# A decoder layer's feed-forward: the last batch in two halves of its tokens, and the previous norm's variance between two units of the projection up

## What is computed

```python
def _layernorm(x, axis=-1, eps=1e-05):
    m = jnp.mean(x, axis=axis, keepdims=True)
    v = jnp.var(x, axis=axis, keepdims=True)
    return (x - m) / jnp.sqrt(v + eps)
...
h = _bitlinear(x, w_fc) + gate * (x @ v.T @ fast_b.T @ u.T)
r = jnp.maximum(h, 0.0)
return _bitlinear(r * r, w_proj)      # w_proj rounded to -1, 0, 1, with one scale for each output row
...
x = _layernorm(x + _L0_ffn_ref(x, ...), axis=-1)
```

## Time and profile before

| | |
|---|---|
| device time, median of 3 runs (lowest, highest) | 1326.9 us (1326.89, 1328.72) |
| time of the profiled execution | 1323.5 us |
| span of its trace | 1321.6 us |
| busy in the span: PE, DVE, ACT, POOL | 1270.6, 923.3, 792.9, 776.1 us |
| granted TensorE clock, mean | 0.988 of full speed |

### The profile page before, as it was taken

One profiled execution on the slowest core, in us unless ns is written; L12 is line 12 of the kernel. 1 busy time (PEld: TensorE's weight loads), 2 busy tenths in 40 slices (PEclk: granted clock), 3 DMA queues, 4 the chain that ended last, 5 costly groups with the idle time before them and its releaser, 6 DMA issues.

```text
span 1321.6 us, 21020 instructions
## 1 busy us (share of the span) xinstructions
PE 1270.6 (96%) x6800; PEld 846.9 (64%) x6800; DVE 923.3 (70%) x1802; ACT 792.9 (60%) x1058; POOL 776.1 (59%) x449
## 2 busy tenths in 40 slices
PE   6999999999999999999999999999999998899995
PEld 4767765657566666756665666666666664677773
DVE  6578876684775777476667757675765678678885
ACT  2353445575666566565656655565666556688983
POOL 3504218994877787677868767794876779200000
PEclk9999999999999999999999999999999999999997
DMA  6301211100200110010011001100100100101100
GB/s 213 112 32 64 82 47 19 19 2 17 50 4 1 32 34 0 16 32 18 0 32 34 0 16 32 18 0 21 44 2 1 48 17 1 48 32 48 48 32 32
DMA packets 99118, 43.07 MB, mean 33 GB/s; under 512 B 77152, under 2 KB 81520, under 8 KB 99072
## 3 DMA queue, kind: packets, MB, share of 16 engines
q1 hardware_dynamic: 98256, 39.33, 11.9%
q0 software_dynamic: 816, 3.15, 0.7%
HBM read 29.59 MB, written 12.58 MB: 32 GB/s over the span
## 4 chain that ended last, share of the span: by engine, by line
PE 89%; POOL 3%; DVE 3%; ACT 2%; issue 1%; SPq 1%; DMA 1%; POOLq 0%; ACTq 0%; DVEq 0%
PE ps L1310 16%; PE ps L1285 14%; PE ps L48 11%; PE ps L50 10%; PE ps L49 10%; PE ps L1301 4%; PE ps L1289 4%; PE ps L1342 2%; PE ps L1344 2%; PE ps L1343 2%; PE ps L1660 2%; PE ps L1661 2%; PE ps L1319 2%; POOL acc L931 2%; PE ps L716 1%
## 5 line engine op out<-in xcount | busy, mean ns | idle before, releaser
L1139 DVE CUSTOM_DVE_ANT_0 junk<-ps,mask 128x512 bf16<-128x512 f32 x504 | 314.9, 686 | 89.1 <-PE ps L1301 87.8
L1005 ACT ACTIVATE prob<-ps,mcol 128x1024 f32<-128x1024 f32 x256 | 281.9, 1116 | 139.5 <-PE ps L1289 134.5
L931 POOL TENSOR_TENSOR acc<-acc,prob 128x1024 f32<-128x1024 f32 x128 | 306.9, 2398 | 11.5
L928 POOL TENSOR_TENSOR acc<-prob 128x1024 f32<-128x1024 f32 x64 | 155.3, 2426 | 219.7 <-ACT prob L1005 218.4
L1310 PE MATMUL ps<-prob,v_b 128*64 128x512 f32 x1024 | 245.0, 599 | 0.2 <-ACT prob L1005 0.2
L945 POOL TENSOR_TENSOR acc_lo<-acc,acc_hi 128x1024 f16<-128x1024 f32 x64 | 138.7, 2167 | 5.1
L1310 PEld LDWEIGHTS ps<-prob,v_b 128*64 128x64 f32 x1024 | 67.9, 137 | 108.1 <-issue 74.9
L1285 PE MATMUL ps<-q_hi,k_hi 64*128 64x512 f32 x512 | 114.8, 444 | 4.2 <-DVE rs L225 4.0
L1301 PE MATMUL ps<-k_hi,q_hi 64*128 64x512 f32 x504 | 100.9, 395 | 3.8 <-DVE nmx L1139 3.8
L1289 PE MATMUL ps<-shift,ones_r 64*128 64x512 f32 x512 | 102.1, 394 | 0.1
L1285 PE MATMUL ps<-q_lo,k_hi 64*128 64x512 f32 x512 | 102.1, 394 | 0.0
(11 more groups left out here) (213 smaller groups left out, 2869.2 us busy)
## 6 DMA issues: line engine op xcount, KB each, us to landing
shift<-nmx SPq DMA_DIRECT2D x512, 0.5 KB, 2.0
x_in<-in_xT SPq DMA_DIRECT2D x8, 512.0 KB, 3.6
x_scratch<-x_a SPq DMA_DIRECT2D x8, 512.0 KB, 2.8
raw<-in_cT SPq DMA_DIRECT2D x8, 512.0 KB, 3.6
raw<-x_scratch SPq DMA_DIRECT2D x8, 512.0 KB, 3.8
y<-x_scratch SPq DMA_DIRECT2D x8, 512.0 KB, 3.7
y_scratch<-y SPq DMA_DIRECT2D x8, 512.0 KB, 2.8
y_c<-y_scratch SPq DMA_DIRECT2D x8, 512.0 KB, 3.8
```

What stands on the lines that cost most here:

```text
L928: pool.tensor_tensor(total, prob[:, 0], prob[:, 1], ALU.add).then_inc(acc_out, 1)
L931: pool.tensor_tensor(total, total, prob[:, kt], ALU.add).then_inc(acc_out, 1)
L1005: act.activation(prob[:, i].rearrange("p h t -> p (h t)"), SCORE[i % 2].rearrange("p h t -> p (h t)"), ACT.Exp, scale=SCALE, bias=mcol[:, ...
L1139: dve.tensor_tensor_reduce(junk[:, t % 2, h], SMAX[t % 2][:, h], mask[:], -1.0, -LOWEST, ALU.add, ALU.min, nmx[:, p % 2, t, h:h + 1]).then ...
```

## The change

In the last batch alone:

- `var3(b - 1)` moves on PE from between the tiles of `project` to between `hidden` 6 and 7, `norm3_root(b - 1)` on ACT to between the units 6 and 7, and the root's part on DVE (`root3`, split off from `normalise3`) to before the last h_lo. The output x3 of batch 6 (`scale3`) stays behind it.
- `project` works on two halves of 256 tokens: twice as many matmuls (64), each of 256 columns and with its own weight load. The early half writes the first 256 columns of the banks in OUT, the late half the last 256 columns of the banks HIDDEN[0] and HIDDEN[1]. The order is: early, both groups, tiles 0 to 5; late, group 0, tiles 0 to 5; early, tiles 6 and 7; late, group 1, tiles 0 to 5; late, tiles 6 and 7.
- The norm of the last batch is made for each half: residual, sum, mean, deviation, squares (now on ACT, not DVE), their sum, variance, root, output, and a store of 256 KB for each half. The statistics of the early half go to bank 0, those of the late half to bank 5.

For all other batches the order of every engine stays what it was.

```diff
@@ sync
-        for b in range(B - 4, B):
+        for b in range(B - 4, B - 1):
             store(b)
-        sp.wait_ge(f.stored, 16 * B)
+        for j, cols in enumerate(HALVES):
+            sp.wait_ge(x3_out, B + j)
+            sp.dma_start(batch_cols(out, B - 1)[:, :, cols], x3[:, :, cols]).then_inc(f.stored, 16)
+        sp.wait_ge(f.stored, 16 * (B + 1))
@@ scalar, batch
-            for i in (6, 7):
-                hidden(b, i, first)
-            if not first:
+            hidden(b, 6, first)
+            if last:
+                norm3_root(b - 1, second)
+            hidden(b, 7, first)
+            if not (first or last):
                 norm3_root(b - 1, second)
@@ scalar, end
-        norm3_root(B - 1, False)
+        def last_squares(j, cols):
+            act.wait_ge(dev3_out, B + j)
+            act.activation(sq3[:, :, cols], dev3[:, :, cols], ACT.Square).then_inc(sq3_out, 1)
...
+        for j, cols in enumerate(HALVES):
+            last_squares(j, cols)
+        for j, cols in enumerate(HALVES):
+            last_root(j, cols)
@@ vector, batch
             hidden_lo(b, 6)
...
+            if last:
+                root3(b - 1)
             hidden_lo(b, 7)
...
+            if not (first or last):
+                root3(b - 1)
             if not first:
-                normalise3(b - 1, second)
+                scale3(b - 1, second)
@@ vector, end
+        early, late = HALVES
+        last_residual(0, early)
+        last_deviation(0, early)
+        last_residual(1, late)
+        last_sum_squares(0, early)
+        last_deviation(1, late)
+        last_sum_squares(1, late)
+        last_normalise(0, early)
+        last_normalise(1, late)
@@ tensor
+        def project_half(j, m, tiles):
+            for k in tiles:
+                pe.wait_ge(f.lo_out, HK * (B - 1) + k + 1)
+                w = f.tern[:, k, m * P:(m + 1) * P]
+                pe.matmul(LAST_OUT[j][m], w, h_hi[:, k, HALVES[j]], start=(k == 0), stop=False)
+                mm = pe.matmul(LAST_OUT[j][m], w, h_lo[:, k, HALVES[j]], start=False, stop=(k == HK - 1))
+            if tiles[-1] == HK - 1:
+                mm.then_inc(f.p_ps, 1)
@@ tensor, batch
+            hidden(b, par, 6, first)
+            if last:
+                var3(b - 1)
+            hidden(b, par, 7, first)
...
+            if last:
+                pe.wait_ge(f.relu_out, HK * b + 6)
+                for m in range(DK):
+                    project_half(0, m, range(0, 6))
+                project_half(1, 0, range(0, 6))
+                for m in range(DK):
+                    project_half(0, m, (6, 7))
+                project_half(1, 1, range(0, 6))
+                for m in range(DK):
+                    project_half(1, m, (6, 7))
@@ tensor, end
-        mean3(B - 1, False)
-        var3(B - 1)
+        for j, cols in enumerate(HALVES):
+            pe.wait_ge(y3_sum_out, B + j)
+            if j == 1:
+                pe.wait_ge(rs3_out, 2 * (B - 1))
+            pe.matmul(LAST_STAT[j], c["mean_w"][:], y3_sum[:, cols], start=True, stop=True).then_inc(mean3_ps, 1)
+        for j, cols in enumerate(HALVES):
+            pe.wait_ge(sq3_sum_out, B + j)
+            pe.matmul(LAST_STAT[j], c["mean_w"][:], sq3_sum[:, cols], start=True, stop=True).then_inc(var3_ps, 1)
```

More of the change, by code:

```diff
@@ L1470, in ffn_phase @@
     y3, dev3, sq3, x3, y3_sum, sq3_sum = f.y3, f.dev3, f.sq3, f.x3, f.y3_sum, f.sq3_sum
+    HALVES = (slice(0, T // 2), slice(T // 2, T))
+    LAST_STAT = tuple(bank[:, cols] for bank, cols in zip((STAT2, STAT3), HALVES))
+    LAST_OUT = tuple([bank[:, cols] for bank in banks] for banks, cols in zip((OUT, HIDDEN[:2]), HALVES))
     @block.sync
@@ L1536, in _, with last_root @@
         batch(B - 1, 1, False, False, True)
-        norm3_root(B - 1, False)
+        def last_squares(j, cols):
+            act.wait_ge(dev3_out, B + j)
+            act.activation(sq3[:, :, cols], dev3[:, :, cols], ACT.Square).then_inc(sq3_out, 1)
+        def last_root(j, cols):
+            est, inv, done = f.est3[:, cols], f.inv3[:, cols], 3 * (B - 1 + j)
+            act.wait_ge(var3_ps, B + j)
+            if j == 0:
+                act.wait_ge(rs3_out, 2 * (B - 1))
+            act.activation(inv, LAST_STAT[j], ACT.Ln, bias=c["eps"][:, 0:1]).then_inc(est3_out, 1)
+            act.wait_ge(est3_out, done + 1)
+            act.activation(est, inv, ACT.Exp, scale=-0.5).then_inc(est3_out, 1)
+            act.wait_ge(est3_out, done + 2)
+            act.activation(inv, est, ACT.Square).then_inc(est3_out, 1)
+        for j, cols in enumerate(HALVES):
+            last_squares(j, cols)
+        for j, cols in enumerate(HALVES):
+            last_root(j, cols)
     @block.vector
@@ L1574, in deviate3, with root3, scale3 @@
                               ALU.subtract).then_inc(dev3_out, 1)
-        def normalise3(b, first):
+        def root3(b):
             f.inverse_root(dve, STAT3, (f.est3, f.inv3, f.rs3), est3_out, rs3_out, b)
+        def scale3(b, first):
             if not first:
@@ L1623, in _, with last_residual, last_deviation, last_sum_squares @@
         batch(B - 1, 1, False, False, True)
[L1624 to L1628, removed]
+        def last_residual(j, cols):
+            for m in range(DK):
+                dve.wait_ge(f.p_ps, 2 * (B - 1 + j) + m + 1)
+                if j == 0 and m == 0:
+                    dve.wait_ge(dev3_out, B - 1)
+                dve.scalar_tensor_tensor(out=y3[:, m, cols], in0=LAST_OUT[j][m], scalar=pscale[:, m:m + 1],
+                                         in1=f.x2[:, 1, m, cols], op0=ALU.mult, op1=ALU.add).then_inc(f.y3_out, 1)
+            dve.wait_ge(f.y3_out, 2 * (B + j))
+            if j == 0:
+                dve.wait_ge(mean3_ps, B - 1)
+            dve.tensor_tensor(y3_sum[:, cols], y3[:, 0, cols], y3[:, 1, cols], ALU.add).then_inc(y3_sum_out, 1)
+        def last_deviation(j, cols):
+            dve.wait_ge(mean3_ps, B + j)
+            if j == 0:
+                dve.wait_ge(x3_out, B - 1)
+            mean = LAST_STAT[j].rearrange("p (o t) -> p o t", o=1).to_broadcast([P, DK, T // 2])
+            dve.tensor_tensor(dev3[:, :, cols], y3[:, :, cols], mean, ALU.subtract).then_inc(dev3_out, 1)
+        def last_sum_squares(j, cols):
+            dve.wait_ge(sq3_out, B + j)
+            if j == 0:
+                dve.wait_ge(var3_ps, B - 1)
+            dve.tensor_tensor(sq3_sum[:, cols], sq3[:, 0, cols], sq3[:, 1, cols], ALU.add).then_inc(sq3_sum_out, 1)
+        def last_normalise(j, cols):
+            f.inverse_root(dve, LAST_STAT[j], (f.est3[:, cols], f.inv3[:, cols], f.rs3[:, cols]), est3_out, rs3_out,
+                           B - 1 + j)
+            if j == 0:
+                dve.wait_ge(f.stored, 16 * (B - 1))
+            rs = f.rs3[:, cols].rearrange("p (o t) -> p o t", o=1).to_broadcast([P, DK, T // 2])
+            dve.scalar_tensor_tensor(out=x3[:, :, cols], in0=dev3[:, :, cols], scalar=-0.5, in1=rs, op0=ALU.mult,
+                                     op1=ALU.mult).then_inc(x3_out, 1)
+        early, late = HALVES
[7 more added lines that the diff above has]
+        last_normalise(1, late)
     @block.tensor
@@ L1680, in batch @@
                 ca.last_project()
-            for i in (6, 7):
-                hidden(b, par, i, first)
+            hidden(b, par, 6, first)
+            if last:
+                var3(b - 1)
+            hidden(b, par, 7, first)
             if first:
@@ L1686, in batch @@
                 pe.wait_ge(f.y3_out, 2 * b)
[L1687 to L1692, removed]
+            if last:
[6 more added lines that the diff above has]
+                project_half(1, 1, range(0, 6))
+                for m in range(DK):
+                    project_half(1, m, (6, 7))
+            else:
+                for m in range(DK):
+                    project(b, m, range(0, 6))
+                if not first:
+                    var3(b - 1)
+                for m in range(DK):
+                    project(b, m, (6, 7))
         pe.wait_ge(f.w_split, DK)
```

## The result

| | before | after |
|---|---|---|
| median of 4 runs each (lowest, highest) | 1326.89 us (1326.21, 1328.72) | 1317.07 us (1315.16, 1319.53) |
| ratio, 95% interval | | 0.9923 [0.9906, 0.9941] |
| profiled execution, its span | 1323.5, 1321.6 us | 1318.0, 1315.9 us |

The change is faster, by 0.8%. The two traces differ by 5.7 us only. Three numbers for one gain: that is the first thing to settle.

What follows compares the result with a forecast made beforehand. PE was taken as the bound (busy 1270.6 of 1321.6 us), then a tail of one-at-a-time whole-tensor operations. Tail start 2.2, store 0.35 and overlapping halves 4.95 make 7.5 us off the median 1326.9: 1319.4, range 1317.3 to 1322.6.

Steps and rivals of the forecast that it cites:

- The mechanism: Last batch's tail: 2.2 us from its earlier start, 4.95 from overlapping halves, 0.35 from the store, 7.5 us less.
- The projection: Last batch on PE: 64 matmuls of 256 columns at 0.114 us each, ending at 1301.8, 0.9 later than before.
- stall at tile 7: PE before tile 7: ACT's root 1 us late makes PE stand, 1320.4; chance 0.84 together with the main forecast.
- The store: End of the kernel: a 256 KB store takes 2.8 us after the last output, 0.35 sooner; bounds 2.45 and 3.3.
- (a): Tail: halves cost nearly what wholes do, handovers 0.1 to 0.2 us; 2 to 3 us back, 1322.4; chance 0.07.
- (b): Projection: a 256-column matmul steps as a 512-column one, 0.227; 7.2 us more on PE, 1326.4, no change; chance 0.05.
- (c): Projection: weight load not hidden behind so short a matmul, 0.30 a pair; 11.9 us more, 1331.3, slower; chance 0.03.
- the clock's terms: Tail statistics on PE: only the late variance at half clock; another fall costs 0.5 us, none gives back 0.5.
- How the numbers follow: Prediction's part setting chances and range: 1317.3 to 1322.6 us; faster 0.91, same 0.05, slower 0.04.

Runs made afterwards that it cites:

- v_alone: The kernel before with only batch 6's variance and its root moved, projection and last norm whole; ratio 0.9977 to the kernel before.
- h_alone: The changed kernel with batch 6's variance and root back behind unit 7, so only the halves remain; ratio 0.9968 to the kernel before.
- r_first: The changed kernel with the late residual and sum ahead of the early deviation on DVE; ratio 0.9944 to the kernel before.
- m_early: The changed kernel with the early mean on PE ahead of the last eight projection matmuls; ratio 0.9945 to the kernel before.
- one_store: The changed kernel with one store of 512 KB behind the late output instead of two of 256 KB; ratio 0.9965 to the kernel before.
- w_warm: The changed kernel with six extra matmuls of 512 columns on PE ahead of the late variance; ratio 0.9960 to the kernel before.

## Why the prediction was wrong, and where it was right

The steps, in the trace after, with the 1.65 us by which its mark stands later taken off:

| step | predicted | after |
|---|---|---|
| variance of batch 6 starts | 1292.25 | 1292.13 |
| h_lo of unit 7 ends | 1298.8 | 1298.76 |
| x of batch 6 starts | 1298.7 | 1298.68 |
| step of a projection matmul | 0.114 | 0.120 ((1303.68 - 1296.13) / 63) |
| early mean starts | 1301.80 | 1302.15 |
| late deviation starts | 1305.1 | 1305.51 |
| late variance | 1.22 | 1.23 |
| late output ends | 1311.3 | 1311.70 |
| from there to the end | 2.8 | 2.55 |
| end | 1314.1 | 1314.25 |

- **The mechanism** stands: v_alone and h_alone show both parts, and the queueing that the forecast named (the late residual behind the early deviation, the early mean behind the projection) is confirmed by r_first and m_early. The tail lost 7.35 us for 7.5 forecast, with the chain 0.4 us later than forecast and the store 0.25 quicker.
- **The projection** was 0.35 us dearer than forecast, the step of 0.120 for 0.114. No stall at tile 7 was seen: its h_lo was done at 1300.41, and PE got there at 1300.69. The Trainium skill, "TensorE: Matmul & The Clock Gate", section "Wait — 56ns, not 53.3ns?", has about 62 ns for a matmul; counted for the load as well, as the prediction did, that is an estimate of 0.124 for a pair. The runs have 0.120 and, for 128 columns, 0.111 over 128 pairs, so at this count it isn't what binds here.
- **The store** gave 0.6 for 0.35, and 0.25 of it went around the span.
- **The rivals** (a), (b) and (c) fell with the handovers of 0.02 to 0.04, the step, and the loads that came every 0.111. Of (b)'s sum, 1319.4 and 7.2 make 1326.6, not 1326.4, which changes nothing. Of the clock's terms the one I took held in this trace; v_alone, h_alone and m_early show others, in which a statistic takes 0.5 to 0.95 more or less.
- **The step that failed** is in "How the numbers follow": "The three runs of before lie 1.8 us apart, so I add 1.2 below and 0.6 above". Three runs were too few to show the spread, and a fourth execution stood beside them: the profiled one, 1323.5, with which the four lie 5.2 us apart. The prediction took its distance for a fixed one and carried it over. Twelve executions of that same kernel spread over 6.3 us (standard deviation 2.0). A median of three or four then is off by about 1 us on either side, and the difference of two by some 1.5. The measured gain of 9.8 is 2.5 above the tail's 7.35. The first four executions of the changed kernel had their median at 1317.07; the 17 later ones, in two comparisons, at 1319.37 and 1318.95. That these lie within 0.5 of the forecast of 1319.4 is luck in part: the kernel before had medians of 1325.8 and 1324.0 beside them, not 1326.9, and the gains were 6.2 and 5.8 us, under the 7.5. Of the tail's 7.35 the 0.25 around the span go off; the intervals (4.6 to 8.0 and 3.7 to 7.8 us) hold the 7.1 that are left. That the larger gain of the first comparison is spread ahead of the mark is what fits all this: its one traced execution of the changed kernel has the same 27.80 us behind the mark as the two later ones, and the 9.8 did not come again. Its other executions have no trace.

## What to carry to other kernels

Here a tail of dependent whole-tensor operations halved well: each half's operation still cost mostly its columns (0.42 us on DVE for 256 columns, 0.69 for 512), and the half matmul stayed just above the floor of a weight load with its matmul; at that floor nearly the whole gain was gone. With two chains in one engine's order, what stands behind a waiting operation decides: move the half that is ready, and then look which half is last, since it changes. And before a range is put around a difference of a few us, take the spread of single executions from many runs, or compare stretches between marks in the trace rather than whole times.

## What was not expected of the hardware

- A pair of 128x128 weight load and matmul of the rounded type took 0.227, 0.120 and 0.111 us for 512, 256 and 128 columns, each at the full clock.
- Executions of one kernel on one core differ by 6 us in 1326. In the traces of one kernel the part behind the mark is the same to 0.02 us (35.15 and 35.17 before; 27.80, 27.78 and 27.80 after), while the mark moves by 2.0 and by 1.3 us. The half-clock stretches of TensorE at the changes of phase come out longer or shorter: 7 or 14 us between 1100 and 1150 us, and none, 3.5 or 7 us between 195 and 220 us (mean granted clock 1.00, 0.93 or 0.86), over the 14 traces.
- In the tail the clock fell 19.0 to 19.6 us behind the mark in five traces with the same work on PE up to there (the three of the changed kernel, one_store and w_warm), read in slices of 0.25 us; that is 3.3 to 3.9 us behind the last projection step. In the two of the kernel before it was 4.5 and 4.9 us behind that step. In m_early it fell only 22.2 us behind the mark. A difference of half a microsecond in the fall decides whether the early variance takes 0.59 or 0.88 us.
- In w_warm the clock came back to full within the tail, behind six extra matmuls of 512 columns that had run at the half clock.
